# Values product of an attention and FFN kernel: high and low values side by side in one 512-column product

## What is computed

```python
Q = xpos(x @ W_Q); K = xpos(x @ W_K, downscale=True); V = x @ W_V
p = softmax(Q @ K.T) * 0.9 ** abs(n - m)
x = layernorm(x + p @ V)
gate, y = q4(x) @ q4(w_gate).T, q4(x) @ q4(w_up).T       # 704 columns each
x = layernorm(x + q4(silu(gate) * y) @ q4(w_down).T)
```

## Time and profile before

| | us |
|---|---|
| median of 3 runs (lowest to highest) | 1038.21 (1037.75 to 1039.31) |
| the profiled execution | 1038.84 |
| its span in the trace | 1037.1 |
| TensorE matmul busy | 1003.4 (97%) |
| VectorE busy | 897.5 (87%) |
| GpSimd busy | 754.0 (73%) |
| ScalarE busy | 581.0 (56%) |

### The profile page before, as it was taken

How to read it: one execution, slowest core, us unless ns; L and a number is a source line. 1 busy time by engine, 2 the same in 40 slices (tenths; PEclk the granted TensorE clock), 3 DMA queues, 4 the chain that set the end, 5 groups by cost and what they waited for, 6 DMA issues and landing times.

```text
span 1037.1 us, 19938 instructions
## 1 busy us (share of the span) xinstructions
PE 1003.4 (97%) x6414; PEld 910.6 (88%) x6414; DVE 897.5 (87%) x1877; ACT 581.0 (56%) x1448; POOL 754.0 (73%) x973
## 2 busy tenths in 40 slices
PE   5799999999999999999999999999999999999996
PEld 4588998999999999999999999999999999989885
DVE  7979888899888889888888988889888888978886
ACT  2554656555565655556655564655556565555543
POOL 5876868768686867868677686876868686766654
PEclk9899999999999999999999999999999999999999
DMA  8020202101111201201021010210111010000000
GB/s 301 1 72 11 63 11 83 41 13 61 42 57 37 61 17 36 83 21 52 21 74 39 22 61 11 82 42 21 52 41 60 34 63 16 16 21 22 21 12 26
DMA packets 28246, 47.21 MB, mean 46 GB/s; under 512 B 2800, under 2 KB 21488, under 8 KB 26224
## 3 DMA queue, kind: packets, MB, share of 16 engines
q1 hardware_dynamic: 27056, 44.64, 13.6%
q10 hardware_dynamic: 1088, 1.31, 0.4%
HBM read 37.55 MB, written 8.39 MB: 44 GB/s over the span
## 4 chain that ended last, share of the span: by engine, by line
PE 83%; POOL 6%; DVE 5%; issue 4%; DMA 1%; ACT 0%; POOLq 0%; SPq 0%; DVEq 0%; ACTq 0%
PE ps_g L471 11%; PE ps_g L473 11%; PE ps_g L472 11%; PE ps_oy L471 8%; PE ps_oy L473 8%; PE ps_oy L472 8%; PE ps_t L480 8%; PE ps_s L471 5%; PE ps_s L472 5%; PE ps_s L473 5%; POOL h L1932 2%; PE ps_oy L480 1%; POOL prob L2029 1%; DMA xin<-x_t 1%; PE ps_oy L612 1%
## 5 line engine op out<-in xcount | busy, mean ns | idle before, releaser
L1932 POOL TENSOR_TENSOR h<-h,hsc 128x704 f32<-128x704 f32 x252 | 202.6, 817 | 59.9 <-DVE h L1426 28.8
L2029 POOL TENSOR_TENSOR prob<-prob,decay_t 128x512 f32<-128x512 f32 x128 | 163.6, 1293 | 5.4 <-ACT prob L973 5.0
L471 PE MATMUL ps_oy<-v_h,pt_h 128*128 128x256 f32 x512 | 150.2, 293 | 1.1 <-DVE first_down L1328 1.1
L471 PE MATMUL ps_g<-wgu_h,xqt_h 128*128 128x480 f32 (+1 forms) x380 | 149.4, 393 | 0.6 <-issue 0.4
L473 PE MATMUL ps_oy<-v_h,pt_l 128*128 128x256 f32 x512 | 144.6, 282 | 0.0
L472 PE MATMUL ps_oy<-v_l,pt_h 128*128 128x256 f32 x512 | 144.6, 282 | 0.0
L473 PE MATMUL ps_g<-wgu_h,xqt_l 128*128 128x480 f32 (+1 forms) x380 | 142.5, 375 | 0.0
L472 PE MATMUL ps_g<-wgu_l,xqt_h 128*128 128x480 f32 (+1 forms) x380 | 142.5, 375 | 0.0
L471 PE MATMUL ps_s<-k_h,q_h 128*128 128x512 f32 x256 | 105.5, 412 | 5.8 <-POOL q_l L1908 5.8
L471 PEld LDWEIGHTS ps_oy<-v_h,pt_h 128*128 128x128 f32 x512 | 97.4, 190 | 4.7 <-DVE pt_l L1444 3.0
L472 PE MATMUL ps_s<-k_l,q_h 128*128 128x512 f32 x256 | 101.1, 395 | 0.0
(11 more groups left out here) (250 smaller groups left out, 3040.6 us busy)
## 6 DMA issues: line engine op xcount, KB each, us to landing
rope_t<-rope SPq DMA_DIRECT2D x15, 1024.0 KB, 5.3
xres<-x SPq DMA_DIRECT2D x64, 128.0 KB, 2.0
out<-yout SPq DMA_DIRECT2D x63, 128.0 KB, 1.7
xin<-x_t SPq DMA_DIRECT2D x15, 512.0 KB, 4.2
first_rope<-rope SPq DMA_DIRECT2D x2, 512.0 KB, 9.5
decay_t<-decay SPq DMA_DIRECT2D x1, 960.0 KB, 14.1
first_down<-w_down SPq DMA_DIRECT2D x1, 704.0 KB, 12.2
first_gate_up<-w_gate SPq DMA_DIRECT2D x2, 256.0 KB, 6.0
```

The source lines that it names most:

```text
L471: pe.matmul(dst, a_h, b_h, start=(start and i == 0), stop=False)
L1932: return tt(blocks(dst), blocks(src), sc[:, which, at:at + n].unsqueeze(2).to_broadcast([P, n, QB]), ALU.mult)
L2029: tt(prob[:, keys], prob[:, keys], decay_t[:, lo:lo + CW], ALU.mult).then_inc(decayed, 1)
```

## The change

1. The four operands of a key tile are no longer given to `product`. `v_h` and `v_l` become the halves of one buffer `v_hl`, and one matmul with `pt_h` over `v_hl[:, :, at:at + D]`, 2 x 256 = 512 columns, writes the whole bank: high x high in `ps_o[:, 0:D]`, high x low in `ps_o[:, D:2D]` (`o_low`). A second matmul of 256 columns adds low x high to the first half.
2. The sum of the halves moves to VectorE: `low_residual` computes xres = o_low * rinv + xres, and `first_residual`, behind it in every step, waits for `low_done` and computes r1 as before.
3. `w_down` and `rope_first`, which are needed at the start only, lie in one buffer `first_home` where `v_hl` comes to lie.
4. The branch of the last batch gets other orders on ScalarE, VectorE and GpSimd.

```diff
@@ -134,10 +134,11 @@
         k_h = sb("k_h", [P, 2 * DH * L], F32R)
         w_last = sb_before("last_gate_up", [P, 2, 2 * D])
         k_l = sb("k_l", [P, 2 * DH * L], F32R)
-        w_down = sb_before("first_down", [P, 2, FP])
-        v_h = sb("v_h", [P, 2 * NT * D], F32R)
-        rope_first = sb_before("first_rope", [P, 4, CW])
-        v_l = sb("v_l", [P, 2 * NT * D], F32R)
+        first_home = sb_before("first_home", [P, 2 * FP + 4 * CW])
+        w_down = first_home[:, 0:2 * FP].rearrange("p (a n) -> p a n", a=2)
+        rope_first = first_home[:, 2 * FP:2 * FP + 4 * CW].rearrange("p (a n) -> p a n", a=4)
+        v_hl = sb("v_hl", [P, 2, 2 * NT * D], F32R)
+        v_h, v_l = v_hl[:, 0], v_hl[:, 1]
         q_h = sb("q_h", [P, 2, DH, CW], F32R)
         q_l = sb("q_l", [P, 2, DH, CW], F32R)
         xt_h = sb("xt_h", [P, DH, CW], F32R)
...
@@ -186,7 +187,8 @@
         ps_o = ps_oy[:, 0]
         ps_y = ps_oy[:, 1]
         r1 = ps_o[:, 0:D]
-        r1_scratch = ps_o[:, D:2 * D]
+        o_low = ps_o[:, D:2 * D]
+        r1_scratch = o_low
         he = ps_t[:].rearrange("p a b n -> p (a b n)")[:, 0:F]
 
 
...
@@ -541,11 +544,14 @@
                         pe.wait_ge(first_vl_done[1], 1)
                     transposes(ps_t[:, g], [prob[:, n * P:(n + 1) * P] for n in range(4 * g, 4 * g + 4)], pt_done)
 
-            def over_keys(i, tiles):
-                def val(t, n):
+            def over_keys(i, tiles, last_inc=None):
+
+                for n in tiles:
                     at = half_of(i // NT) * (NT * D) + n * D
-                    return t[:, at:at + D]
-                return [(pt_h[:, n, :], pt_l[:, n, :], val(v_h, n), val(v_l, n)) for n in tiles]
+                    pe.matmul(ps_o, pt_h[:, n, :], v_hl[:, :, at:at + D], start=n == 0, stop=False)
+                    mm = pe.matmul(ps_o[:, 0:D], pt_l[:, n, :], v_h[:, at:at + D], start=False, stop=n == NT - 1)
+                if last_inc is not None:
+                    mm.then_inc(last_inc, 1)
 
             def values_product_first(i):
                 if live(i):
...
@@ -557,13 +563,13 @@
 
                         pe.wait_ge(first_vl_done[0], 1)
                         pe.wait_ge(wgrid_done, BLOCKS)
-                    product(ps_o[:, 0:D], over_keys(i, range(NT // 2)), None, stop=False)
+                    over_keys(i, range(NT // 2))
 
             def values_product_second(i):
                 if live(i):
 
                     wait(pe, ptl_done, 2 * i + 2)
-                    product(ps_o[:, 0:D], over_keys(i, range(NT // 2, NT)), o_done, start=False)
+                    over_keys(i, range(NT // 2, NT), o_done)
 
             def x1_transposes(i):
                 if live(i):
...
@@ -1160,18 +1166,18 @@
                     tanh(dn, 2)
                     x_magnitude(gu)
                     probs_high(prev, 0)
+                    probs_high(prev, 1)
                     r2_squares(end)
-                    probs_high(prev, 1)
                     x1_high(gu)
                     h_magnitude(dn)
                     r1_mean(prev)
+                    if turned is not None:
+                        rotated_high(*turned)
                     r1_squares(prev)
+                    tanh(gu, 0)
                     exponential(now)
-                    tanh(gu, 0)
                     output(end)
                     h_high(dn, 0)
-                    if turned is not None:
-                        rotated_high(*turned)
                     h_high(dn, 1)
                 else:
                     x_magnitude(gu)
...
@@ -1475,12 +1481,17 @@
                     nc.vector.tensor_reduce(nmax[:, i % 2:i % 2 + 1], ps_s[:].rearrange("p a n -> p (a n)"), AX_X,
                                             ALU.max, negate=True).then_inc(max_done, 1)
 
-            def first_residual(i):
+            def low_residual(i):
                 if live(i):
                     wait(dve, rinv_done, i + 1)
                     wait(dve, xres_in, 16 * (i + 1))
                     wait(dve, o_done, i + 1)
-
+                    stt(out=xres[:], in0=o_low, scalar=rinv[:, 0:1], in1=xres[:],
+                        op0=ALU.mult, op1=ALU.add).then_inc(low_done, 1)
+
+            def first_residual(i):
+                if live(i):
+                    wait(dve, low_done, i + 1)
                     stt(out=r1, in0=r1, scalar=rinv[:, 0:1], in1=xres[:],
                         op0=ALU.mult, op1=ALU.add).then_inc(r1_done, 1)
 
...
@@ -1704,6 +1718,7 @@
                     xqt_low(gu)
                     v_low(c_v, 1)
                     h_shift(dn)
+                    low_residual(prev)
                     first_residual(prev)
                     h_grid(dn)
                     row_max(now)
...
@@ -1760,12 +1776,13 @@
                     row_max(now)
                     xqt_low(gu)
                     row_inverse(prev)
+                    low_residual(prev)
                     first_residual(prev)
                     h_shift(dn)
                     h_grid(dn)
+                    gated(gu, 0)
                     first_norm(prev)
                     x_max(prev)
-                    gated(gu, 0)
                     x_scales(prev)
                     silu(gu, 0)
                     second_residual(fin)
...
@@ -2145,12 +2165,12 @@
                     x_units(prev)
                 elif s // NT == NB - 1:
                     r2_variance(end)
-                    r2_inverse(end)
                     x_quantised(gu)
-                    r2_shift(end)
                     if turned is not None:
                         rotate(*turned, 1)
                     h_units(dn)
+                    r2_inverse(end)
+                    r2_shift(end)
                     r1_variance(prev)
                     r1_inverse(prev)
                     h_quantised(dn, 0)
...
@@ -2158,9 +2178,9 @@
                     h_quantised(dn, 1)
                     decay_half(now, 0)
                     x_units(prev)
+                    decay_half(now, 1)
                     if turned is not None:
                         rotated_low(*turned)
-                    decay_half(now, 1)
                 else:
                     x_quantised(gu)
                     if turned is not None:
```

More of the change, by code:

```diff
@@ L241, in build @@
         rinv_done = sem("rinv_done")
+        low_done = sem("low_done")
         r1_done = sem("r1_done")
@@ L1630, in _ @@
             weight_low(4)
+            low_residual(0)
             first_residual(0)
@@ L1649, in _ @@
             xqt_low(0)
+            low_residual(1)
             first_residual(1)
@@ L1820, in _ @@
             xqt_low(last - 2)
+            low_residual(last - 1)
             first_residual(last - 1)
@@ L1845, in _ @@
             h_reciprocals(last - 2)
+            low_residual(last)
             first_residual(last)
```

## The result

The changed kernel took 1049.70 us (median of 4 runs, 1049.61 to 1050.74), the kernel before, on the same chip, 1038.76 us (1037.75 to 1039.87). The ratio is 1.0107, with a 95% interval of 1.009 to 1.0125: slower by 10.9 us.

A forecast was written before the change was run, and what follows sets the result against it. TensorE's stream was taken to set the time for nine tenths of the span. Terms -6.2 + 4.9 + 2.7 + 0.3 - 1.2 + 0.5 + 0.5 gave +1.5 us on 1038.2, so 1039.7 us, range 1033.0 to 1044.0.

The forecast's parts named there:

- The products: Values product on TensorE: one 512- and one 256-column matmul save 0.012 us per tile, 6.2 us over 512 tiles.
- The bound of 0.340: Values product: if every pair of matmuls took 0.340 us per tile, the gain would be 10.2 us.
- The added instruction: VectorE's low_residual ahead of first_residual: r1 comes 0.44 to 0.52 us later, taken as 0.46.
- Rotation steps: 27 loop steps: h_transposes(dn, 1) has room 0.34, needs 0.46; stall 0.12 plus restart 0.06, 4.9 us lost.
- the rival for the slower side: r1 delayed by 0.52 us: rotation steps lose 6.5, j = 4 steps 3.0; total 1042.7 us, chance 0.22.
- The step after j = 3: Projection waiting for silu(dn, 2): room 0.09, stall 0.37, the first of seven pays 0.46; 2.7 us lost.
- Steps j = 1 and 5: Room before h_transposes(dn, 1) is about 0.05 us; 0.3 us lost for all these steps.
- Steps j = 7, last batch, tail: j = 7: VectorE's idle time swallows the delay; last batch steps 58 to 62 nil; tail at h_transposes(last - 3) 0.5 us.
- New orders of the last batch: Step 57: the 1.91 us wait for decay_half(now, 1) goes, h_quantised comes later; net gain 1.2 us (0 to 2).
- Opening: first_residual(1) leads through tanh and silu to a wait within the listed 0.9 us; 0.5 us lost.
- The faster rival: Rooms of 0.34 us hold the delay, rotation steps lose nothing; 1032.9 us, chance 0.28 with times from 1032 to 1036.

The follow-up runs named there:

- product_alone: The changed kernel without low_residual: high x low is computed into o_low but not added, first_residual waits for TensorE again; 1033.34 us, ratio to before 0.9947.
- silu_earlier: The changed kernel with gated(gu, 0) ahead of first_norm and silu(gu, 0) ahead of x_scales in steps j = 1 and 5; 1047.34 us, ratio 1.0082.

## Why the prediction was wrong, by its steps

The table by stretch gives what each part was worth: the product -3.7 us (3.00 in steps 8 to 55, 0.33 in the opening, 0.06 and 0.28 behind), low_residual +16.0 (after less product_alone, without the time ahead of step 1: 1.97 + 12.97 + 0.25 + 0.79), the orders -1.5. Together +10.8, against the 10.9 between the medians. The forecast had -6.2, +8.9 and -1.2.

- **The products: right in kind, too large.** A pair takes 0.235 + 0.117 = 0.352 us in the median where three took 0.360: 0.008 a tile, not 0.012. The bound of 0.340 wasn't met. By the formula in the Trainium skill, TensorE: Matmul & The Clock Gate, section Back-to-back issue gap, it would have been an estimated 1.3 us; the measured 3.7 lies between it and the forecast. That page gives the formula for an isolated matmul and says itself that it is off in a stream of weight loads and matmuls, a condition that the prediction left out.
- **The added instruction: right in kind, mis-sized.** 0.484 + 0.04 = 0.52 us of delay, where the upper bound was 0.52 and I took 0.46. The row I leaned on, x_shift of 0.414 us, has a constant as scalar; the nearer one was first_residual itself, 0.49, with the same column. The Trainium skill, SBUF — State Buffer, section Who interferes with whom, was borne out: the 64 low_residuals took 0.484 us in the median and none more than 0.487, though GpSimd was at work beside 51 of them.
- **Rotation steps: the wait right, the size off.** 27 steps lost 6.4 us (0.24 each), not 4.9. The missing 0.06 is that of the instruction; the rival for the slower side gave 6.5 by this very number. The stall is 0.19 and the restart 0.055 (a transpose behind a stall has its successor after 0.165 us and not 0.11), as forecast.
- **The step after j = 3: right, a little small.** silu(dn, 2) is what the projection waits for; 7 steps lost 3.5 us, not 2.7, again for the 0.06 and a restart of 0.04.
- **Steps j = 1 and 5: the step of the working that failed.** The prediction looked at one customer of the delayed chain, h_quantised and the transposes, and put 0.3 us down for all 14 steps. silu(gu, 0) stands behind first_norm, x_max and x_scales in VectorE's queue there, and gate_up(gu, 2) can't start without it: it ended 0.34 us before that matmul in the kernel before, too little for 0.46 as well as for 0.52. These steps lost 4.2 us. 3.2 of them are that wait, as silu_earlier shows, and it is the largest part of the 7.1 by which the instruction was under-priced. The other 1.0 is the wait that was looked at, at the transposes of h. Its line doesn't hold together either: a room of 0.05 us against a need of 0.46 would give 5.7 us, not 0.3. The trace of the kernel before has GpSimd done 0.54 us before the fifth transpose of h in such a step (297.74 and 298.28), so 0.05 can only be what is left of the room behind the delay.
- **Steps j = 7, last batch, tail: near.** The instruction costs 0.03 us in a step j = 7; 0.3 in the steps 57 to 62, where I had nil, and 0.46 in step 63, where I had 0.5.
- **New orders of the last batch: right.** They gave 1.5 us where I had 1.2 (0 to 2).
- **Opening: one wait of two.** Steps 1 and 2 lost 0.9 us and not 0.5: in step 1 the transposes of the down weights now wait 0.4 us for VectorE's wd_l. VectorE itself waits there for ScalarE's wd_h, which stands behind r1_mean and r1_squares in ScalarE's queue and starts 0.44 us later in the step.

Of the rivals, the slower one (0.22) had the right delay and said 1042.7; with the steps j = 1 and 5 at their 4.2 us, and the products at 3.7, it would have come to 1042.7 + 3.3 + 2.5 = 1048.5. So no rival had the wait that made the difference. The faster rival, that rooms of 0.34 us hold a delay of 0.40, was never near.

## What to carry to other kernels

Where one engine's stream is full and the others are timed to it within a third of a microsecond, a new instruction on a chain costs in every step whatever the nearest room doesn't hold, and here shedding matmuls didn't pay it back: 0.52 us of delay in each of 64 steps cost 16 us, and 3.7 were gained. For each instruction put into a queue, list all that stands behind it and the customer of each, with its room, before pricing one of them; here the one left out was the largest part of the error, 3.2 of 9.4 us. And price a new instruction by a row with the same kinds of operands, scalars included.

## What the runs showed of the hardware beyond that

- A [128, 1] column as the scalar of a VectorE instruction on 256 elements costs 0.06 us over a constant: 0.484 against 0.425 us, 47 and 48 instructions.
- `x_scales`, a TENSOR_SCALAR on 128x16 elements from SBUF to SBUF, ends with the two-input instruction of GpSimd that it starts beside: 62 of the 64 in the changed kernel end 0.03 to 0.04 us behind one, after 0.19 to 1.27 us, and the two that started beside none took 0.17 and 0.18. The RECIPROCAL on the same 128x16 elements isn't held (0.23 to 0.26 us, with GpSimd at work or not). h_low put ahead of it cost nothing where x_scales stayed beside the same instruction of GpSimd (steps j = 3), and 0.66 us where that moved it beside the next one (step 3).
- For the moving operand of a matmul, two runs of 256 columns 4096 elements apart are as good as 512 adjacent ones: 0.235 and 0.234 us to the next start.
